# Experts' hidden rows: split into two bf16 parts before they are turned, and turned by DMA transposes instead of by TensorE

## The reference, cut to what matters

```python
    logits = x @ Wr + br
    probs = jax.nn.softmax(logits, axis=-1)
    top_w, top_idx = jax.lax.top_k(probs, 1)
    g = jnp.einsum('td,edf->tef', x, Wg)
    u = jnp.einsum('td,edf->tef', x, Wu)
    h = jax.nn.silu(g) * u
    y = jnp.einsum('tef,efd->ted', h, Wd)
    sel = jnp.take_along_axis(y, top_idx[:, :, None], axis=1)[:, 0]
    out = sel * top_w
```

## Time and profile before

| | us |
|---|---|
| median of 3 runs (653.93 to 662.95) | 654.2 |
| the profiled execution | 651.07 |
| its span, first to last instruction | 649.0 |
| TensorE busy in the span | 561.3 |
| mean granted TensorE clock over the span, of 2.4 GHz | 0.964 |

### The profile page before, as it was taken

The page is one execution under the profiler, slowest core; times in us unless marked ns, Lnnn a source line. Parts: engine busy times, 40 slices in busy tenths (PEclk is TensorE's granted clock), DMA queues, the critical chain, the costliest instruction groups (busy, mean ns, idle before and its releaser), DMA issues. The chain is left out here.

```text
span 649.0 us, 15220 instructions
## 1 busy us (share of the span) xinstructions
PE 561.3 (86%) x5090; PEld 339.2 (52%) x5123; DVE 393.2 (61%) x812; ACT 332.3 (51%) x622; POOL 118.9 (18%) x162
## 2 busy tenths in 40 slices
PE   3798999999989999997888888851899999999991
PEld 1344555555546665554555555531466656666661
DVE  1677989898986334554988888876134333432331
ACT  2366677777755244448888888830222221222120
POOL 3302222222602000000000000002132332233211
PEclk9999999999999999997999999985899999999997
DMA  8865555554760000006866666641111111111110
GB/s 283 220 122 150 126 126 125 124 129 112 154 160 11 0 1 1 1 1 162 201 157 155 154 160 159 157 122 17 33 36 38 48 47 30 33 49 40 36 31 3
DMA packets 29414, 60.30 MB, mean 93 GB/s; under 512 B 5989, under 2 KB 16647, under 8 KB 26952
## 3 DMA queue, kind: packets, MB, share of 16 engines
q1 hardware_dynamic: 20624, 25.68, 13.5%
q0 software_dynamic: 6432, 18.46, 13.2%
q10 hardware_dynamic: 2328, 15.75, 10.2%
HBM read 58.75 MB, written 7.81 MB: 103 GB/s over the span
## 5 line engine op out<-in xcount | busy, mean ns | idle before, releaser
L1311 DVE TENSOR_REDUCE nmax<-PB 128x2 f32<-128x512 f32 x128 | 85.6, 682 | 20.8 <-PE PB L854 19.1
L539 ACT ACTIVATE probs<-PC 128x512 f32<-128x512 f32 x128 | 73.9, 609 | 20.4 <-PE PC L866 19.4
L783 ACT CAST probs<-PC 128x1024 bf16<-128x1024 f32 x19 | 19.2, 1012 | 113.6 <-PE PC L1222 113.6
L1747 DVE TENSOR_TENSOR probs<-PC,probs 128x1024 bf16<-128x1024 f32 x19 | 23.3, 1225 | 80.9 <-ACT probs L783 80.9
L1214 PE MATMUL PA<-arena,probs 128*128 x227 | 54.4, 391 | 7.6 <-issue 3.9
L854 PE MATMUL PB<-small 64*128 64x256 bf16 x256 | 51.1, 291 | 6.6 <-DVE nmax L1311 6.5
L1233 PE MATMUL PD<-arena,probs 128*128 x456 | 52.9, 273 | 2.5 <-issue 2.5
L1214 PE MATMUL PB<-arena,probs 128*128 x210 | 48.6, 379 | 0.9
L1233 PEld LDWEIGHTS PD<-arena,probs 128*128 128x128 bf16 x456 | 44.2, 98 | 8.3 <-issue 3.2
L454 POOL DMA_DIRECT2D arena<-in_w_all x16 | 8.5, 532 | 206.9 <-DVE arena L1588 120.0
L866 PE MATMUL PC<-small 64*128 64x256 bf16 x256 | 45.8, 281 | 0.5 <-DVE small L1327 0.5
(11 more groups left out here) (213 smaller groups left out, 1099.8 us busy)
## 6 DMA issues: line engine op xcount, KB each, us to landing
arena<-idx_low ACTq DMA_DIRECT2D x15, 1024.0 KB
wst<-in_w_all SPq DMA_DIRECT2D x48, 256.0 KB, 2.8
arena<-in_w_all POOLq DMA_DIRECT2D x16, 384.0 KB, 5.4
arena<-in_idx_all SPq DMA_DIRECT2D x1, 2176.0 KB, 10.2
arena<-in_cond SPq DMA_DIRECT2D x16, 128.0 KB, 7.8
small<-in_x SPq DMA_DIRECT2D x16, 128.0 KB, 10.3
arena<-idx_low POOLq DMA_DIRECT2D x2, 1024.0 KB, 15.0
tok_r<-rows SPq DMA_DIRECT2D x1, 2048.0 KB, 16.9
```

What stands on the lines that cost most here:

```text
L539: nc.scalar.activation(probs[:, c, o], PC[:, o], ACT.Exp, scale=SCALE0).then_inc(S["ex"], 1)
L1311: v.tensor_reduce(nmax[:, c, s, :], PB[:, s * 512:(s + 1) * 512].rearrange("p (a k) -> p a k", k=T), AX.X, ALU.max, negate=True).then_inc( ...
```

## The change

- The split into a high and a low bf16 part is made on the hidden rows as they are, before they are turned. ScalarE's `rounded` (L797 in the changed kernel) rounds `hh` (SBUF) to `h_high`; VectorE's `low_rows` (L1752) writes hh - h_high to `h_low`. The semaphores are `hr` and `hs`. There is one `h_high` and one `h_low`, so both also wait for the DMA that still reads them.
- SyncE turns them: `turn_hidden` issues two DMA transposes a tile (L383), 128x1024 bf16 each (256 KB), from SBUF to SBUF, high then low, into `hT[par]`, of which there are now two (`probs[:, 2, :]` and the new `turned_odd`). 38 of them in all, in one order on one queue. Each waits for `hr` or `hs` of its tile, and for the `down` of two tiles earlier.
- `turn_h` is gone from TensorE, and PC is not used in this stage any more. `down` waits for `turned_high` and `turned_low` of its tile.
- The first tiles' order changes a little: `tile_in(1)` stands ahead of the up product of tile 0.
- On ScalarE and VectorE the step on tile j's hidden rows now stands in the turn of tile j, behind `gate(j)` and `x_high(j + 1)`, or `hidden_rows_of(j)` and `x_low(j + 1)`, and no longer at the head of tile j + 1.

```diff
@@ -265,13 +265,15 @@
         bsel = sb("bsel", [P, B, 2, SLOTS], BF16)
         tokn = sb("tokn", [P, SLOTS], I32)
         small_at[0] = 0
+        turned_odd = part([P, FF])
         xin = part([P, 2, T])
         xres = part([P, 2, REST])
         asel = part([P, B, P], BF16)
         eq = part([P, B, SLOTS])
 
         gs, hh = probs[:, 0, :], probs[:, 1, :]
-        hT_hi, hT_lo = (probs[:, 2, n * 512:(n + 1) * 512].bitcast(BF16) for n in range(2))
+        hT = [b.bitcast(BF16).rearrange("p (a f t) -> p a f t", a=2, f=FT) for b in (probs[:, 2, :], turned_odd)]
+        h_high, h_low = (part([P, FF], BF16) for n in range(2))
         xT_hi, xT_lo = (probs[:, 3, n * T:(n + 1) * T].bitcast(BF16).rearrange("p (n t) -> p n t", n=2) for n in range(2))
         yo = probs[:, 3, 512:1024].rearrange("p (n t) -> p n t", n=2)
 
...
-            "xld0", "xld1", "res0", "res1", "tT", "th", "tl", "gu", "gs", "uu", "hm", "hT", "hTh", "hTl", "y", "yo", "so0", "so1")
+            "xld0", "xld1", "res0", "res1", "tT", "th", "tl", "gu", "gs", "uu", "hm", "hr", "hs", "turned_high0", "turned_high1", "turned_low0", "turned_low1", "y", "yo", "so0", "so1")
@@ -372,6 +374,16 @@
                 keep_tokens(b)
             sp.wait_ge(S["rows"], 1)
             sp.dma_start(tok_r[0:TOK, T:REST].rearrange("(b p) t -> p b t", p=P), rows[:, :, 2 * T:ROW], allow_slow_non_contiguous=True).then_inc(S["wkept"], 16)
+
+            def turn_hidden(j, par):
+                for a, (src, done, turned) in enumerate(((h_high, "hr", "turned_high"), (h_low, "hs", "turned_low"))):
+                    sp.wait_ge(S[done], j + 1)
+                    if j >= 2:
+                        sp.wait_ge(S["y"], j - 1)
+                    sp.dma_start(hT[par][:, a], src, transpose=True).then_inc(S[f"{turned}{par}"], 16)
+
+            for j in range(SLOTS):
+                turn_hidden(j, j % 2)
 
 
         @block.gpsimd
@@ -777,28 +789,28 @@
                 unless_first(act, S["hm"], j)
                 nc.scalar.activation(gs, PA[:], ACT.Silu).then_inc(S["gs"], 1)
 
-            def h_high(j):
-                act.wait_ge(S["hT"], j + 1)
-                unless_first(act, S["y"], j)
-                nc.scalar.copy(hT_hi, PC[:]).then_inc(S["hTh"], 1)
-
-            def tile(j, par, more=True):
-                h_high(j - 1)
+            def rounded(j, par, half):
+                act.wait_ge(S["hm"], j + 1)
+                if not (isinstance(j, int) and j < 1):
+                    act.wait_ge(S[f"turned_high{1 - par}"], 16 * half)
+                    act.wait_ge(S["hs"], j)
+                nc.scalar.copy(h_high, hh).then_inc(S["hr"], 1)
+
+            def tile(j, par, half, more=True):
                 gate(j)
                 if more:
                     x_high(j + 1, 1 - par)
+                rounded(j, par, half)
 
             x_high(0, 0)
-            gate(0)
-            x_high(1, 1)
-            tile(1, 1)
-            tile(2, 0)
+            tile(0, 0, 0)
+            tile(1, 1, 1)
+            tile(2, 0, 1)
             with act.Fori(1, (SLOTS - 2) // 2) as u:
-                tile(2 * u + 1, 1)
-                tile(2 * u + 2, 0)
+                tile(2 * u + 1, 1, u + 1)
+                tile(2 * u + 2, 0, u + 1)
             for j in range(SLOTS - 2 + (SLOTS % 2 == 0), SLOTS):
-                tile(j, j % 2, j + 1 < SLOTS)
-            h_high(SLOTS - 1)
+                tile(j, j % 2, (j + 1) // 2, j + 1 < SLOTS)
 
 
         @block.tensor
@@ -1215,22 +1227,15 @@
                             k += 1
                 ins.then_inc(S[done], 1)
 
-            def turn_h(j):
-                pe.wait_ge(S["hm"], j + 1)
-                unless_first(pe, S["hTl"], j)
-                for f in range(FT):
-                    ins = pe.transpose(PC[:, f * P:(f + 1) * P], hh[:, f * P:(f + 1) * P], ident)
-                ins.then_inc(S["hT"], 1)
-
-            def down(j, e):
-                pe.wait_ge(S["hTh"], j + 1)
-                pe.wait_ge(S["hTl"], j + 1)
+            def down(j, half, par, e):
+                pe.wait_ge(S[f"turned_high{par}"], 16 * half + 16)
+                pe.wait_ge(S[f"turned_low{par}"], 16 * half + 16)
                 unless_first(pe, S["yo"], j)
                 k = 0
                 for f in range(FT):
                     o = bass.ds(e * (FT * T) + f * T, T)
-                    for v, w in ((hT_hi, wd_hi), (hT_hi, wd_lo), (hT_lo, wd_hi)):
-                        ins = mm(PD[:, 512:512 + T], v[:, f * P:(f + 1) * P], w[:, o], start=(k == 0), stop=(k == 3 * FT - 1))
+                    for a, w in ((0, wd_hi), (0, wd_lo), (1, wd_hi)):
+                        ins = mm(PD[:, 512:512 + T], hT[par][:, a, f, :], w[:, o], start=(k == 0), stop=(k == 3 * FT - 1))
                         k += 1
                 ins.then_inc(S["y"], 1)
 
@@ -1239,16 +1244,15 @@
 
             def tile(j, half, par, more=True):
                 gate_up(j, par, expert_of(j), PA, wg_hi, wg_lo, "gs", "gu")
-                turn_h(j - 1)
                 gate_up(j, par, expert_of(j), PB, wu_hi, wu_lo, "hm", "uu")
                 if more:
                     tile_in(j + 1, half + par, 1 - par)
-                down(j - 1, expert_of(j - 1))
+                down(j - 1, half + par - 1, 1 - par, expert_of(j - 1))
 
             tile_in(0, 0, 0)
             gate_up(0, 0, expert_of(0), PA, wg_hi, wg_lo, "gs", "gu")
+            tile_in(1, 0, 1)
             gate_up(0, 0, expert_of(0), PB, wu_hi, wu_lo, "hm", "uu")
-            tile_in(1, 0, 1)
             tile(1, 0, 1)
             tile(2, 1, 0)
             with pe.Fori(1, (SLOTS - 2) // 2) as u:
@@ -1256,8 +1260,7 @@
                 tile(2 * u + 2, u + 1, 0)
             for j in range(SLOTS - 2 + (SLOTS % 2 == 0), SLOTS):
                 tile(j, j // 2, j % 2, j + 1 < SLOTS)
-            turn_h(SLOTS - 1)
-            down(SLOTS - 1, expert_of(SLOTS - 1))
+            down(SLOTS - 1, (SLOTS - 1) // 2, (SLOTS - 1) % 2, expert_of(SLOTS - 1))
 
 
         @block.vector
@@ -1735,16 +1738,18 @@
                 dve.wait_ge(S["th"], j + 1)
                 v.tensor_tensor(xT_lo[:, par, :], PD[:, 0:T], xT_hi[:, par, :], ALU.subtract).then_inc(S["tl"], 1)
 
-            def hidden(j):
+            def hidden_rows_of(j):
                 dve.wait_ge(S["gs"], j + 1)
                 dve.wait_ge(S["uu"], j + 1)
-                unless_first(dve, S["hT"], j)
+                unless_first(dve, S["hr"], j)
+                unless_first(dve, S["hs"], j)
                 v.tensor_tensor(hh, PB[:], gs, ALU.mult).then_inc(S["hm"], 1)
 
-            def h_low(j):
-                dve.wait_ge(S["hTh"], j + 1)
-                unless_first(dve, S["y"], j)
-                v.tensor_tensor(hT_lo, PC[:], hT_hi, ALU.subtract).then_inc(S["hTl"], 1)
+            def low_rows(j, par, half):
+                dve.wait_ge(S["hr"], j + 1)
+                if not (isinstance(j, int) and j < 1):
+                    dve.wait_ge(S[f"turned_low{1 - par}"], 16 * half)
+                v.tensor_tensor(h_low, hh, h_high, ALU.subtract).then_inc(S["hs"], 1)
 
             def result(j, par, half, back):
                 dve.wait_ge(S["y"], j + 1)
@@ -1754,25 +1759,23 @@
                 v.scalar_tensor_tensor(out=yo[:, par, :], in0=PD[:, 512:512 + T], scalar=xres[:, par, T:T + 1],
                                        in1=xres[:, par, 0:T], op0=ALU.mult, op1=ALU.add).then_inc(S["yo"], 1)
 
-            x_low(0, 0)
-            hidden(0)
-            x_low(1, 1)
-
-            def tile(j, par, half, back, more=True):
-                h_low(j - 1)
-                hidden(j)
+            def tile(j, par, half, back, after, more=True, before=True):
+                hidden_rows_of(j)
                 if more:
                     x_low(j + 1, 1 - par)
-                result(j - 1, 1 - par, half, back)
-
-            tile(1, 1, 0, False)
-            tile(2, 0, 0, False)
+                low_rows(j, par, after)
+                if before:
+                    result(j - 1, 1 - par, half, back)
+
+            x_low(0, 0)
+            tile(0, 0, 0, False, 0, before=False)
+            tile(1, 1, 0, False, 1)
+            tile(2, 0, 0, False, 1)
             with dve.Fori(1, (SLOTS - 2) // 2) as u:
-                tile(2 * u + 1, 1, u, True)
-                tile(2 * u + 2, 0, u, True)
+                tile(2 * u + 1, 1, u, True, u + 1)
+                tile(2 * u + 2, 0, u, True, u + 1)
             for j in range(SLOTS - 2 + (SLOTS % 2 == 0), SLOTS):
-                tile(j, j % 2, (j - 1) // 2, True, j + 1 < SLOTS)
-            h_low(SLOTS - 1)
+                tile(j, j % 2, (j - 1) // 2, True, (j + 1) // 2, j + 1 < SLOTS)
             result(SLOTS - 1, (SLOTS - 1) % 2, (SLOTS - 1) // 2, True)
 
 
```

## The result

The changed kernel took 636.1 us (median of 4 runs, 632.4 to 637.5), the kernel before 658.6 (653.9 to 663.0) in the runs beside it. Some executions of a kernel here run one to two per cent longer than its others, and the ratio compares the fast ones only. It is 0.9707, 95% interval 0.967 to 0.9743: 2.9% faster, where 1.6% was forecast. The profiled execution took 637.0 us, its span is 635.2.

A forecast was written before the change was run, and what follows sets the result against it. TensorE alone was taken to bound the experts' stage. Removed turns (-16.6 us), first-tile and last-turn waits moved down(18) by -13.2; a lower clock added 2.5: -10.7, giving 643.5 us median, range 640 to 691.

The forecast's parts named there:

- down(0) to down(17), 17 tiles: Experts' stage loop: each tile loses the TensorE turn, 0.87 + 0.05 = 0.92 us; -15.6 us over this stretch.
- up product's end to down(18): End of the program, where nothing covers the last DMA turn: 8.3 us in place of 6.14, so +2.2.
- down(18) at a lower clock: Last down product: after a 5.6 us pause it runs at 1.2 GHz for nearly all its work, +2.5 us.
- the tile would then take 9.35 - 0.92 = 8.43 us: Each tile of the experts' stage: only the turn's 0.92 us leaves TensorE's path, all else staying the same.
- L: Time from the end of a tile's up product to its low transpose's landing: forecast 8.3 us, cover 8.65.
- d: Time from issue to landing of one 256 KB DMA transpose on SyncE's queue, taken as 4.4 us.
- The lower bound: Landing of a DMA turn, bounded from below by a plain 256 KB load on the same queue: 2.8 us.
- rival B: DMA queue: transposes queue behind each other at a cost per packet and downs wait; 667 to 692 us, chance 0.27.
- o: Time the high transpose occupies the DMA queue ahead of the low one: 0.9 us, which doesn't count up to 1.3.
- A: DMA turns: as cheap as a plain copy, landing after 2.8 us; 638 to 641 us, chance 0.13.
- The bound for two per cent faster: Whole kernel: over 2% faster needs the up product's end to the low transpose's landing under 6.6 us; chance 0.13.
- C: DMA turns: 128x128 blocks go one after another, 12.8 us a turn, 25.6 a tile; about 970 us, chance 0.13.

The follow-up runs named there:

- e1: Kernel before, with TensorE's turn of the previous tile moved ahead of the gate product; ratio to the kernel before 0.988.
- e2: Changed kernel, with the 8 TensorE transposes kept between gate and up beside the DMA turns, their output unread; ratio to the kernel before 0.9875.
- e10: Kernel before, with TensorE's loop over tiles 3 to 16 written out; one run, 647.6 us against 648.8 for the kernel before beside it.
- e4: Changed kernel, with two more DMA transposes a tile between high and low, into unread spare buffers; ratio to the kernel before 1.044.
- e7: Changed kernel without the low transposes, the down product reading the turned high part in their place; one run, 639.4 us.
- e5: Changed kernel, with one 128x2048 DMA transpose a tile in place of two of 128x1024; ratio to the kernel before 0.989.
- e3: Changed kernel, with one more DMA transpose a tile between high and low, into an unread spare buffer; ratio to the kernel before 1.012.
- e9: Changed kernel, with down's high-part matmuls first and the last tile turned by TensorE; ratio to the kernel before 0.965.

## Why the prediction was wrong

The direction was right, and so was what is taken off the path and what is put on it; the size was not: -10.7 us forecast, -18.3 in the stage. Term by term, with the stage's pieces read from both chains:

| piece | forecast | measured |
|---|---|---|
| first gather to down(0) | +0.3 | -1.0 (20.56 to 19.61) |
| down(0) to down(17), 17 tiles | -15.6 | -20.1 (158.36 to 138.30) |
| up product's end to down(18) | +2.2 | +1.0 (6.14 to 7.17) |
| down(18) at a lower clock | +2.5 | +1.7 (2.81 to 4.49) |
| sum | -10.6 | -18.3 |

**The step that failed** is "the tile would then take 9.35 - 0.92 = 8.43 us". It kept the gap of 0.29 ahead of the gate as a fixed part of the tile. It wasn't: I had read it as "what the sum leaves" and not asked what ended it. The row to ask was in the timeline before, VectorE's L1747 ending just ahead of down. The change moves the release of the down product from 0.5 us ahead of its start to 1.0 us in the loop's odd tiles and 1.3 to 1.7 in its even ones (an estimate: every low transpose taken to land 3.23 us behind its issue, as the last did). All the gaps that are left stand behind the downs of odd tiles, where the loop turns. 0.23 of gap and 0.10 of the gate a tile went with it, 5.3 us over 17 tiles by the table's second line (20.1 less 17 turns of 0.87). The 0.05 behind the turn, 0.9 us of the forecast, stayed, so that line is off by 4.5. e1 and e2 show the cause by an earlier release with all the turns in place, e10 by the loop taken out at the same late release, e4 by a slower product ahead of the gate.

**The size of L.** The forecast took d = 4.4 from the DMA in 4 B runs; a turn landed in 3.05 alone and 3.23 behind another, nearer to the plain copy's 2.8. The lower bound was the better row: a turn moves some 1024 packets of 256 B, and neither pieces of 4 B nor the 8192 of 32 B that rival B was priced by. L came to 7.2 in place of 8.3, which takes 1.1 from the end and the wait of 1.0 from the first tile. The time for which the high turn holds up the low one, o, was put at 0.9; it was 1.3 of issue (not in the trace before) and 1.35 of the DMA engines. Since the low part is ready just 1.3 us behind the high one, this cost at most the 0.2 between 3.05 and 3.23.

**The rivals.** A (as cheap as a copy, 638 to 641) came nearest, with a chance of 0.13, and its own price was too small by the same gap. That 636.1 lies on A's side is not because A's mechanism held: L was 7.2, between A's 6.6 and the forecast's 8.3. The bound for two per cent faster, L under 6.6, is 6.9 by the prediction's own sum, and with the gap gone 7.2 was enough. B did not decide here, but its mechanism, turns queueing behind each other, is real: at three turns a tile it took all of the gain. C is excluded: the 8 blocks of a turn land together in 3.05 us. So the 1309 ns for a 128x128 block on the Trainium skill's page (VectorE: DVE Perf Modes, The three transpose paths) is no rate for larger turns; 8 of them took 2.3 times as long as one by that page. The 261 GB/s of the Trainium skill's other page (DMA: Bandwidth & Descriptors, Latency and other measured facts) is nearer, yet above what the runs show: 256 KB in 1.35 us of all engines is 194 GB/s, and 256 KB more in one transpose added 1.2 us, 218 GB/s.

**The clock** fell behind the last pause, of 4.6 us, and cost 1.7 of the 2.5. That it would fall was forecast rightly, when it would fall was not. By the row of the program's end before, 2.5 us behind the last matmul, it would have fallen in the middle of the pause; it stood at 1.00 through all of it and fell 5.3 us behind the last matmul, some 0.7 us into down(18), and it was back before the 24 matmuls were through. Its first matmuls and its last ran at the full clock, so the +2.5 was too much.

Moves forecast at no cost (rounding, low part, result step, SyncE) cost none.

## What to carry to other kernels

A gap labelled "issue" ahead of a product is not a fixed part of a loop: look how long before the need the wait ahead of it is released, because the sequencer's loop and register work hides behind the array only if it has a lead. When a step is taken off the path, count what its earlier release frees as well, and try the reordering alone first (moving one line gave nearly half of the gain). A DMA turn was worth it here where 8 us of other products covered it; at the end of the program, where nothing does, the engine's own turn was faster and kept the clock.

## What the runs showed of the hardware

- A DMA transpose of 128x1024 bf16 from SBUF to SBUF costs SyncE 1.23 to 1.34 us to issue and lands 3.05 us behind its issue when alone (e7); 128x2048 costs 1.9 and 4.25 (e5). Turns in a row land 1.5 to 1.9 us apart (the ends of e3 and e4), slower than they are issued.
- Behind a down of 2.81 us that was released with no lead (e3), TensorE's gap before the next product was 0.71 to 0.95 us where the loop turned, against 0.5 at a lead of 0.5 us (before); behind one of 4.1 us and more (e4) there was none. The product behind a gap took 2.76 in place of 2.59 us.
- Writing TensorE's loop out (e10) took 0.33 us off each tile of the kernel before, the gaps and a part of the gate's 0.17, although the waits were released no earlier.
- The granted clock can fall after the pause that stands ahead of it: 1.00 through 4.6 us without a matmul and for 0.5 us of the next product, then 0.50 (changed kernel). Around pauses of 1.2 us (e9), 1.7 and 1.8 (e3) and 2.4 (before) it stayed at 1.00.
